# A two-layer decoder on one core: residual slots, the second layer's weight set-up moved into the tail of the mixing stage, and the first stage's loads ahead of its stores

## The reference

```python
x = LN(x + recurrent(x))        # x: 2 x 1024 x 256; 1024 sequential steps over a 4-block 32x32 state
x = LN(x + cross_attn(x, ctx))  # 16 heads of 16, 77 context rows
x = LN(x + mu_moe(x))           # entmax-1.5 gate over 16 experts (sort, power), gelu
x = LN(x + self_attn(x))        # 16 heads of 64, 1024 x 1024 scores
x = LN(x + cross_attn(x, ctx))
x = LN(x + fp4_ffn(x))          # weights and activations quantised in blocks of 16, hidden 704

# recurrent, one step t, per batch and block (softmax weights w over the top 2 of 4 blocks):
S_upd = tanh(beta_t * S + (v_t - S @ kn_t) * kn_t^T)
S     = (1 - w) * S + w * S_upd
out_t = sum_blocks sm * (S @ q_t)**2 * sigmoid(S @ q_t)
```

## Time and profile before

| | |
|---|---|
| median of 3 runs | 3188.46 us (3174.97 to 3189.74) |
| profiled execution | 3187.25 us, span 3185.5 us |
| first stage (`project`) | from 0 to about 112 us |
| mixing stage, steps / tail | to about 1570 us / to about 1668 us |
| self attention | to about 2565 us |
| `prepare` | to about 2622 us |
| second layer | to 3185.5 us |
| busy share PE / DVE / ACT / POOL | 67% / 68% / 55% / 21% |

### The profile page before, as it was taken

One profiled execution on the slowest core, in us unless ns is written; L12 is line 12 of the kernel. 1 busy time (PEld: TensorE's weight loads), 2 busy tenths in 40 slices (PEclk: granted clock), 3 DMA queues, 4 the chain that ended last, 5 costly groups with the idle time before them and its releaser, 6 DMA issues. The chain is left out here.

```text
span 3185.5 us, 41817 instructions
## 1 busy us (share of the span) xinstructions
PE 2136.5 (67%) x11068; PEld 1196.0 (38%) x11068; DVE 2168.2 (68%) x10065; ACT 1752.2 (55%) x5691; POOL 654.1 (21%) x343
## 2 busy tenths in 40 slices
PE   5333644556464555546558999999999927777686
PEld 2222433434343333434443333333333314445353
DVE  4899999989999998999724555555555462534535
ACT  2578888888888888888623444444444411121121
POOL 0000000000000000000013666666666700000000
PEclk8655565565666556565668999999999957877787
DMA  3622222222222222222000000000000021011000
GB/s 94 143 53 58 49 59 48 64 47 54 57 49 59 48 63 47 64 48 64 19 4 4 12 16 15 13 12 15 15 13 12 11 68 62 7 33 40 0 7 7
DMA packets 86782, 123.30 MB, mean 39 GB/s; under 512 B 17445, under 2 KB 65225, under 8 KB 86601
## 3 DMA queue, kind: packets, MB, share of 16 engines
q1 hardware_dynamic: 86600, 121.37, 16.0%
HBM read 100.33 MB, written 21.00 MB: 38 GB/s over the span
## 5 line engine op out<-in xcount | busy, mean ns | idle before, releaser
L1417 ACT ACTIVATE mix_cand<-mix_pre,mixer_cbuf 128x32 f32<-128x32 f32 x2048 | 593.0, 290 | 185.2 <-DVE mix_pre L1352 100.9
L1414 ACT ACTIVATE mix_cand<-mix_state,mixer_cbuf 128x32 f32<-128x32 f32 x2048 | 652.6, 319 | 31.5 <-DVE mix_state L1344 3.1
L1339 DVE SCALAR_TENSOR_TENSOR mix_prod<-mixer_keys,mixer_cbuf,mix_cand 128x65 f32<-128x65 f32 x2048 | 581.4, 284 | 53.2 <-ACT mix_cand L1417 47.0
L1844 DVE TENSOR_REDUCE self_tops<-self_rough 128x2 f32<-128x1024 f32 x256 | 311.6, 1217 | 411.5 <-PE self_rough L1616 411.5
L1352 DVE SCALAR_TENSOR_TENSOR mix_pre<-mixer_keys,mix_gap,mix_state 128x32 f32<-128x32 f32 x2048 | 525.4, 257 | 28.0
L1344 DVE SCALAR_TENSOR_TENSOR mix_state<-mix_cand,mixer_cbuf 128x32 f32<-128x32 f32 x2048 | 506.3, 247 | 0.0
L1830 POOL TENSOR_TENSOR self_psum<-self_psum,self_prob 128x1024 f32<-128x1024 f32 x192 | 451.2, 2350 | 160.6 <-ACT self_prob L1757 151.2
L1446 PE MATMUL mix_out<-all_ident,mix_state 128*128 128x128 f32 x512 | 160.6, 413 | 448.0 <-ACT mix_flat L1400 394.5
L1757 ACT ACTIVATE self_prob<-self_sco 128x1024 f32<-128x1024 f32 x256 | 261.5, 1024 | 118.8 <-PE self_sco L1629 104.8
L1453 PE MATMUL mix_out<-mixer_qbd,mix_flat 128*128 128x4 f32 x1024 | 208.4, 335 | 144.7 <-ACT mix_flat L1400 144.7
L858 POOL TENSOR_TENSOR mix_st_norm_rstd<-mix_st_norm_var,mix_half 128x2 f32<-128x2 f32 x24 | 16.7, 697 | 1370.9 <-DVE mix_st_norm_var L851 1370.9
(11 more groups left out here) (392 smaller groups left out, 3313.1 us busy)
## 6 DMA issues: line engine op xcount, KB each, us to landing
mixer_keys<-k_rows SPq DMA_DIRECT2D x256, 260.0 KB, 4.9
aT_rows<-self_aT SPq DMA_DIRECT2D x32, 256.0 KB, 2.3
two_aT<-aT_rows SPq DMA_DIRECT2D x8, 1024.0 KB, 8.3
coef_rows<-mixer_coef SPq DMA_DIRECT2D x4, 1280.0 KB, 6.6
mixer_cbuf<-coef_rows SPq DMA_DIRECT2D x64, 80.0 KB, 5.5
k_rows<-mixer_krow SPq DMA_DIRECT2D x32, 65.0 KB, 3.9
proj_xin<-in_xT SPq DMA_DIRECT2D x8, 256.0 KB, 4.7
mix_st_xin<-in_x SPq DMA_DIRECT2D x8, 256.0 KB, 5.6
```

The lines of the kernel that those rows point to most:

```text
L1339: dve.scalar_tensor_tensor(prod[:, b, :], keys[:, h, b, s_, :], coef(NIB, h, s_, b), cand[:, b, s % 2, :], ALU.mult, ALU.mult, accum_out=g ...
L1414: act.activation(cand[:, b, (s + 1) % 2, NS:2 * NS], state[:, hp, sp_, b, :], ACT.Copy, scale=cbuf[:, h, KEEP, b, s_:s_ + 1]).then_inc(kep ...
L1417: act.activation(cand[:, b, (s + 1) % 2, 0:NS], pre[b], ACT.Tanh, scale=cbuf[:, h, BETA, b, s_:s_ + 1]).then_inc(c_ready[b], 1)
L1844: dve.tensor_reduce(tops[:, kh, t, :], rough[:, :, :], AX.X, ALU.max).then_inc(rough_taken, 1)
```

## The change

Six things, in the order of the program.

- In `project`, `load(1)` is issued ahead of `store(0)`, and from then on `load(g + 2)` ahead of `store(g)`.
- In the slots of `StepLayer`: the queries' two halves, and the residual matmuls after `HEED1` and after `Z1`, get slots of their own; a dozen numbers of the table move by half a slot to two slots; some ACT slots move by one.
- Buffers of the layer (`prob`, `rden`, `aT`, `hT`, `zT` ...) take the room of the first stage's row buffers, which are free once its stores have landed. Each reader of them stands behind one wait for that.
- The second layer's weights are loaded by SP during the mixing stage, after chunk 2. PE computes the second cross-attention's keys and values in the first round (slot 84), ACT copies them (slot 90).
- DVE quantises the FP4 weights and lays out the context weights in the tail, 58 instructions in ten pieces: (slot, count) as in `Later.GAPS`.
- `prepare` is gone. The FP4 transposes (PE) and copies (ACT) stand at the start of the second layer's block, while its first loads run.

```diff
@@ project, SP
             load(0)
+            sp.wait_ge(in_ready, 1)
+            load(1)
             for g in range(NG):
-                if g < NG - 1:
-                    sp.wait_ge(in_ready, g + 1)
-                    load(g + 1)
+                if g < NG - 2:
+                    sp.wait_ge(in_ready, g + 2)
+                    load(g + 2)
@@ StepLayer
-    MIX, READ1, TURN1, ASK, ROUGH, TOP, SCORE0, SCORE1 = 20, 26, 34, 37, 42, 44.5, 52, 60
-    HEED0, RDEN0, HEED1, RDEN1, OUT, READ2, TURN2, GATE, SORT = 60.5, 67, 68, 71.5, 74, 76.5, 84, 87, 91
-    A_TURN, G, Z0, H, Z1, READ3, TURN3 = 113, 116, 118, 119, 128, 131, 138.5
+    MIX, READ1, TURN1, ASK, ROUGH, TOP, SCORE0, SCORE1 = 20, 26, 34, 37, 42, 45.5, 52, 60
+    HEED0, RDEN0, HEED1, RDEN1, OUT, READ2, TURN2, GATE, SORT = 60.5, 66.5, 67, 70.5, 74, 78.5, 86, 89, 93
+    A_TURN, G, Z0, H, Z1, READ3, TURN3 = 113, 115, 117, 118, 127, 132, 139.5
...
         for f in range(KT):
+            yield self.ASK + 2 * f
...
         for j in range(B):
+            yield self.HEED1 + 3.5 + 3 * j
             pe.matmul(self.norm2.y[j], w.ones[0:1, 0:P], w.bvo[:, 1, :], start=True, stop=False)
             pe.matmul(self.norm2.y[j], self.ident[:, :], self.x[:, j, :], start=False, stop=False)
         for f in range(KT):
-            yield (self.OUT - 3, self.OUT)[f]
+            yield self.OUT + f
...
         for n in range(4):
-            yield self.H + 4.5 + n
+            yield self.H + 4 + n
...
+        yield self.Z1 + 0.5
         for j in range(B):
             pe.matmul(self.norm3.y[j], self.ident[:, :], self.x[:, j, :], start=True, stop=False)
@@ new
+class Later:
+    GAPS = ((3, 7), (19.5, 2), (25.5, 2), (45, 7), (66, 10), (77, 14), (91.5, 4), (108.5, 4), (116.5, 2), (126.5, 6))
...
+    def dve(self, dve, spare):
+        steps = self.dve_steps(dve, spare)
+        for slot, n in self.GAPS:
+            yield slot
+            for _ in range(n):
+                next(steps, None)
+        for _ in steps:
+            pass
@@ mix_layer, SP, DVE, ACT, PE
             for c in range(NCH - 2):
+                if c == 3:
+                    later.load(sp, *later_in)
...
-            beside.until(2 * T)
+            rest = Beside((T, later.dve(dve, keys[:, :, :, :, :].rearrange("p h b s j -> p (h b s j)"))))
+            for half_step in range(2 * ROUND + 60):
+                rest.until(T + half_step / 2)
+                beside.until(T + half_step / 2)
...
+                yield 90
+                later.context.setup_act(act)
...
+                yield 84
+                pe.wait_ge(context.k_ready, 1)
+                later.context.setup_pe(pe)
@@ second_layer
-        prepare(nc, context, fp4, xattn_w, ctxT, mask, ffn_w)
...
         def _(pe):
+            fp4.setup_pe(pe)
             pe.wait_ge(w_loaded, 16)
...
         def _(act):
+            fp4.setup_act(act)
```

More of the change, by code:

```diff
@@ L1242, in dve, with __init__, setup_room, load @@
         yield from self.norm3.dve(dve, i, link, self.READ3)
+class Later:
+    GAPS = ((3, 7), (19.5, 2), (25.5, 2), (45, 7), (66, 10), (77, 14), (91.5, 4), (108.5, 4), (116.5, 2), (126.5, 6))
+    def __init__(self, room, ident, ones, blockmask, headmask):
+        self.context = ContextWeights(room, "xa", True, ident, ones, blockmask, headmask)
+        self.fp4 = Fp4Weights(room)
+    def setup_room(self, room, banks):
+        self.context.setup_room(room, "ctx1_", banks)
+        self.small = QuantiseRoom.small(room.sb, "ff", Fp4Weights.FT * D)
+    def load(self, sp, xattn_w, ctxT, mask, ffn_w):
+        self.fp4.load(sp, *ffn_w)
+        self.context.load(sp, *xattn_w, ctxT, mask)
+    def dve_steps(self, dve, spare):
+        ends = 0
+        n = Fp4Weights.FT * D
+        work = QuantiseRoom(spare[:, 0:n], spare[:, n:2 * n], *self.small)
+        fp4, link = self.fp4, Links(dve, self.fp4.set)
+        for ins, last in fp4.setup_dve_steps(dve, work):
+            if last:
+                ends += 1
+                ins.then_inc(fp4.quantised, 1)
+                dve.wait_ge(fp4.quantised, ends)
+            else:
+                link(ins)
+            yield
+        link = Links(dve, self.context.set)
+        for ins in self.context.setup_dve_steps(dve):
+            link(ins)
+            yield
+    def dve(self, dve, spare):
[6 more added lines that the diff above has]
+            pass
 def mix_layer(nc, ident, ones, blockmask, headmask, steps_in, gate_rows, qbd, w_last, x_in, w_outT, xattn_w, ctxT, mask, ffn_w,
-              x_rows, xT_all, w_qkv, w_pair):
+              x_rows, xT_all, w_qkv, w_pair, later, later_in):
     FLIPS = CH * B * NS // P
@@ L1271, in mix_layer @@
         pre_ready = [sem(f"pre_ready{b}") for b in range(B)]
-        context = ContextWeights(room, "xa", False, banks, ident, ones, blockmask, headmask)
-        context.setup_room(room)
+        context = ContextWeights(room, "xa", False, ident, ones, blockmask, headmask)
+        context.setup_room(room, "ctx_", banks)
+        later.setup_room(room, banks)
         experts = EntmaxWeights(room, "ff")
-        layer = StepLayer(room, banks, acc, context, experts, ident, half, root, wout, xT_all, read_summed)
+        layer = StepLayer(room, banks, acc, context, experts, ident, half, root, wout, xT_all, read_summed, steps_in)
         ctx.callback(room.clear_sems)
@@ L1960, in setup_pe @@
                 n += 1
+        pe.wait_ge(self.taken, n)
     def setup_act(self, act):
@@ L2119, in dve, with second_layer @@
         link.close()
-def prepare(nc, context, fp4, xattn_w, ctxT, mask, ffn_w):
-    with ExitStack() as ctx:
-        room = Room(nc, ctx, "prep")
-        context.setup_room(room)
-        fp4.setup_room(room)
-        block = ctx.enter_context(nc.Block())
-        @block.sync
-        def _(sp):
-            fp4.load(sp, *ffn_w)
-            context.load(sp, *xattn_w, ctxT, mask)
-        @block.tensor
-        def _(pe):
-            context.setup_pe(pe)
-            fp4.setup_pe(pe)
-        @block.scalar
-        def _(act):
-            context.setup_act(act)
-            fp4.setup_act(act)
-        @block.vector
-        def _(dve):
-            fp4.setup_dve(dve)
-            context.setup_dve(dve)
-def second_layer(nc, ident, ones, blockmask, headmask, x_rows, aT_rows, w_o, xattn_w, ctxT, mask, ffn_w, out):
+def second_layer(nc, ident, later, x_rows, aT_rows, w_o, out):
     CT = AH * AD // P
@@ L2273, in program @@
         blockmask, headmask = room.sb("blockmask", [P, HF]), room.sb("headmask", [P, HF, P])
+        later = Later(Room(nc, ctx, "late"), ident, ones, blockmask, headmask)
+        later_in = ([a["x1_w" + c] for c in "qkvo"] + [a["x1_b" + c] for c in "qkvo"], a["ctxT"], a["mask1"],
+                    [a["w_gate"], a["w_up"], a["w_down"]])
         keep_ctx = ExitStack()
```

91 lines of the change are left out of this document (50 added, 41 removed).

## The result

The changed kernel takes 3074.05 us (median of 4 executions, 3068.63 to 3077.11) against 3188.43 us (4 executions, 3174.97 to 3189.74): ratio 0.9649, 95% interval 0.9618 to 0.9679. The forecast was 3080, its range 3062 to 3106. The profiled execution took 3077.02 us, 110.2 less than that of before.

What follows compares the result with a forecast made beforehand. VectorE (DVE) was taken to bound the steps, and a chain from engine to engine the tail. From the profiled 3187.25 us, -14.8 - 40.4 + 0.7 + 3.4 - 56.6 gave 3079.55, thus 3080 us, range 3062 to 3106.

Steps and rivals of the forecast that it cites:

- First stage: Loads issued ahead of stores remove DVE's two waits on PE, 15.1 us, less 0.3 for short waits: -14.8 us.
- Slots: Seven rounds beside the steps: reordered slots remove 47.4 us of DVE waits, less an allowance of 7.0: -40.4 us.
- The residual's 17.1: Residual matmuls behind `HEED1` no longer hold up a state part, so ACT's and DVE's waits go: 17.1 us gained.
- the allowance of 7.0: Slots of the layer: thinner margins make DVE wait 1.0 us a round, 7.0 in all, against the gain.
- Set-up: First round: context matmuls at slot 84 cost 0, ACT's four copies at slot 90 cost DVE 0.72: +0.7 us.
- Tail: 58 fills enter DVE's idle times; all fit but two, and the residual behind the read-out adds 0.3: +3.4 us.
- The fourteen fills: Tail, slot 77: 4.4 us of fills in 1.5 us idle, ahead of `BN_STATS`, cost 2.9 us.
- Start of the second layer: `prepare`'s 57 us go; PE's transposes, 8.4 us, are covered by the wait for loads: -56.6 us.
- Rival 1: Waits come back elsewhere in the rounds: -15 instead of -40.4 us, time 3105; chance 16%.
- Rival 2: Fills lie on the tail's chain, +8 instead of 3.4, and second layer's start is uncovered, -48: 3093; chance 11%.
- Rival 4: Slower than before: PE's hold at slot 113 for the sort lasts a chunk, 160 us in all, 3240; chance 1%.
- Rival 3: Tail: by the skill's shared-port rule a fill waits for POOL's power, adding 2.0 us, time 3082; chance 5%.

Runs made afterwards that it cites:

- slots_only: Kernel before with only the changed slot table and the layer's five new or moved yields; 3141.32 us, ratio 0.9854.
- loads_only: Kernel before with only the first stage's two loads issued ahead of the stores; 3172.01 us, ratio 0.9946.
- again: The changed kernel executed once more with nothing changed; 3074.41 us, ratio 0.9656 to the kernel before.
- z_back: Changed kernel with `H`, `Z1` and the yields around the expert matmuls as before, no residual slot there; 3091.02 us, ratio 0.9716 to the kernel before.
- fills_behind: Changed kernel with all 58 fills in one piece behind the layer's last instruction; 3114.77 us, ratio 0.9771 to the kernel before.
- top_back: Changed kernel with `TOP` at slot 44.5 again instead of 45.5; 3085.69 us, ratio 0.9692 to the kernel before.
- fill77_moved: Changed kernel with the fourteen fills at slot 77 moved to the pieces at 91.5 and 108.5; 3073.62 us, ratio 0.9648 to the kernel before.

## Why the prediction was right

- **First stage**, right in its mechanism, 1.9 us too small. It allowed 0.3 for new short waits; 0.9 of old ones went instead. The other 0.8, mostly TensorE's clock in the first group, differs between executions and not between kernels.
- **Slots**, right in the sum (-40.4 forecast, -41.4 by slots_only alone) and partly wrong in its parts. `TOP` gave 8.5 for 10.2, `H` and `Z1` 16.6 for 15.4, each within the noise of the steps. The residual's 17.1 was mis-sized and misattributed: the step "in the new order one part stands ahead of all four ... so the wait goes" names a cure that isn't needed, and "ACT's list is only shifted" passes over the other, the exponentials one slot earlier. Undone together they cost 12.3. Part of the size is again the execution: the same instruction list gave seven such stalls of 17.1 us in the profile before and of 19.9 in loads_only. The queries' 4.7 weren't tried alone. Of the allowance of 7.0, slots_only used 6.0 (47.4 less 41.4); the profile shows it as 2.8 at L1183 in the changed kernel, fuller stalls at the gelu's table (1.54 for 1.38) and some of 0.2 to 0.3.
- **Set-up**: 0.72 at slot 90 and nothing at slot 84, as forecast; the 2.3 that the stall at slot 34 lost is TensorE's clock. No term of the prediction had it.
- **Tail**: wrong in its mechanism, and hidden in the total by the steps' error. +3.4 forecast, +7.7 in the profiled execution, +4.4 in another of the same kernel (107.51). The step that failed is the silent one: that TensorE's clock in the tail would be that of the profiled execution before. Its level at the heads is worth 6.5 us. The fourteen fills, 2.9 forecast, cost 2.3 to 2.9 at the upper level and 0 at the lower, since DVE's wait on PE, the 1.5 of the earlier trace rows there, is 5.7 at the lower (loads_only). 0.4 lies at the first norm, where the residual stands behind the read-out; but that norm starts 11.67 us behind the last step in the profile before and 13.63 in loads_only, with one instruction list, so the 0.3 forecast for it can't be told from the clock. The sign "about 101 us behind the last step" was also counted to 1668, where the stage runs to 1673.10; by its own terms it should have read 106.5, and 110.77 came.
- **Start of the second layer**: -56.7 for -56.6; the cover is real, 7.6 us if it is gone (8.4 forecast).
- **Range and chances**: the low end doesn't follow from its parts, which give 3057 to 3058 and not 3062; the chances of forecast and rivals, all but 1% of them inside the range, don't fit the 15% left outside; and no row gives the 0.4 between the 57 of the earlier trace rows and the 56.6. None of it touches the result, which lies well inside.
- **Rival 1** (-15 instead of -40): excluded. **Rival 2** has its sign in the tail, but not its reason: the tail is as long without fills. **Rival 4**: no wait of DVE in the steps comes from a hold of PE at slot 113.
- **Rival 3**, the shared port. POOL's power and the fills beside it in the tail, POOL, then DVE in time:

```profile
1589.06 5.43 POOL L1149 TENSOR_TENSOR mix_st_sq<-mix_st_delta,mix_root 128x32 f32<-128x32 f32 x1 [3.75 <-DVE mix_st_delta L1239]
```
```profile
1588.90 0.31 DVE L643 TENSOR_TENSOR late_xa_keys<-mix_ctx_kT,mix_ctx_odd 128x154 f32<-128x154 f32 x1
1589.24 0.42 DVE L644 TENSOR_TENSOR late_xa_vals<-mix_ctx_v,all_headmask 77x256 f32<-77x256 f32 x1
1589.70 0.80 DVE L641 TENSOR_TENSOR late_xa_rough_keys<-mix_ctx_kT,all_blockmask 128x616 bf16<-128x616 f32 x1
...
1601.42 0.42 DVE L644 TENSOR_TENSOR late_xa_vals<-mix_ctx_v,all_headmask 77x256 f32<-77x256 f32 x1
```

Two-input instructions start and finish during the power, in the same 0.42 us as without it, and the power keeps its 5.43 of the earlier trace rows. The Trainium skill ("SBUF — State Buffer", section "Who interferes with whom") says that such a pair contends for the shared port, an exclusive lock that makes the later one wait. This trace doesn't agree: neither waited for the other.

## What to carry to other kernels

When two edits both move work away from the same wait, undo each alone and both together before either gets the credit. A piece of filler work is free only between the handovers for which it was cut; one slot's shift of the instruction beside it, from one side of them to the other, put 8.4 us on the chain. On a chain through TensorE, price every matmul at both clock levels, and compare tails of two executions only after looking at the duration of one and the same matmul. Profile the unchanged program twice before a difference of a few us is explained.

## What the runs showed of the hardware that was not expected

TensorE's clock level at a given place is no property of the program. With the same instruction list in the tail, 16 matmuls of L949 took 1.04 us in one execution (kernel before) and 1.93 in another (loads_only); with all of the program the same, 1.93 (after) and 1.05 (again). The first stage and the set-up of the first round show the same, with 3 us (15.1 to 18.4 at the first wait) and 2.3 us between executions. Tails at the upper level lasted 103 to 107.5 us (z_back, slots_only and the kernel before among them), at the lower 110.8 to 113.1; fills_behind and top_back, with their fills placed otherwise, are left out. The lower level held even while PE was busy without a gap, in loads_only:

```profile
1602.33:1616.33 14.00, 14.00 (x156) 0.50 0.00 1
```

and the upper level, for nearly the whole of a stretch of the same length, while it was idle 4.1 of 14 us, in fill77_moved:

```profile
1561.61:1575.61 14.00, 9.90 (x148) 0.98 0.00 1
```

What decides between them at this place stays open. Thirteen executions of the kernel before, beside the first four experiments, lay between 3174.34 and 3194.57 us; the tail's 8.6 us may be a part of that spread, but one profile for each kernel can't show it.
